# Attention scores in a fused three-layer kernel: from split float32r products to plain float32 in four array tiles

## The reference, cut to what matters

```python
q = proj(hidden_states, Wq, bq) * scaling     # 16 heads of 8
k = proj(hidden_states, Wk, bk)
v = proj(hidden_states, Wv, bv)
scores = jnp.einsum('bhsd,bhtd->bhst', q, k)
scores = scores + chunk_attention_mask(S)[None, None]
probs = jax.nn.softmax(scores, axis=-1)
out = jnp.einsum('bhst,bhtd->bhsd', probs, v)
```

## Time and profile before

| | us |
|---|---|
| median of 3 runs | 1470.39 |
| the profiled execution's own time | 1470.57 |
| its span in the trace | 1468.7 |
| PE busy | 1401.1 (95%) |
| DVE busy | 968.2 (66%) |
| ACT busy | 772.3 (53%) |
| POOL busy | 575.4 (39%) |

### The profile page before, as it was taken

The page is one execution under the profiler, slowest core; times in us unless marked ns, Lnnn a source line. Parts: engine busy times, 40 slices in busy tenths (PEclk is TensorE's granted clock), DMA queues, the critical chain, the costliest instruction groups (busy, mean ns, idle before and its releaser), DMA issues.

```text
span 1468.7 us, 27670 instructions
## 1 busy us (share of the span) xinstructions
PE 1401.1 (95%) x10772; PEld 1220.7 (83%) x10772; DVE 968.2 (66%) x2232; ACT 772.3 (53%) x1043; POOL 575.4 (39%) x517
## 2 busy tenths in 40 slices
PE   4898999999899999999999989999999999999998
PEld 3787878888788888787888878888888888888887
DVE  7666787674766757667575776757755666676543
ACT  6555647553565555636465564555634554355321
POOL 4260655443433553247421672146603431352000
PEclk9899999999999999999999999999999999999999
DMA  7111431104110420152004500061004200500000
GB/s 233 50 31 34 133 76 31 30 8 132 24 46 15 137 40 2 45 139 46 8 2 128 100 1 9 18 165 47 1 1 123 40 2 1 150 13 1 1 8 8
DMA packets 84045, 76.32 MB, mean 52 GB/s; under 512 B 5676, under 2 KB 62044, under 8 KB 83916
## 3 DMA queue, kind: packets, MB, share of 16 engines
q1 hardware_dynamic: 83884, 74.55, 19.3%
q10 hardware_dynamic: 32, 0.02, 0.0%
HBM read 61.69 MB, written 12.85 MB: 51 GB/s over the span
## 4 chain that ended last, share of the span: by engine, by line
PE 75%; DVE 10%; issue 5%; POOL 4%; ACT 3%; DMA 0%; DVEq 0%; POOLq 0%; ACTq 0%
PE pd L1135 25%; PE pg L289 7%; PE pu L289 7%; PE pu L290 6%; PE pu L291 6%; PE pg L291 6%; PE pg L290 6%; PE att_ps L760 3%; DVE h L1244 2%; POOL arena L711 2%; PE att_ps L782 1%; DVE x L1232 1%; POOL arena L713 1%; DVE arena L664 1%; DVE ffn_rows L312 1%
## 5 line engine op out<-in xcount | busy, mean ns | idle before, releaser
L1195 ACT ACTIVATE h<-pg 128x512 f32<-128x512 f32 x512 | 304.1, 597 | 645.1 <-PE pg L291 642.7
L1135 PEld LDWEIGHTS pd<-w_down,h 128*128 128x128 f32 x3840 | 480.3, 192 | 30.1 <-issue 3.6
L1135 PE MATMUL pd<-w_down,h 128*128 128x128 f32 x3840 | 494.6, 277 | 1.2 <-DVE x L1232 1.1
L1244 DVE TENSOR_TENSOR h<-h,pu 128x512 f32<-128x512 f32 x512 | 344.0, 677 | 205.0 <-PE pu L291 194.5
L289 PE MATMUL pg<-ffn_x_hi,w_gate_hi 128*128 128x512 f32 (+1 forms) x544 | 249.7, 459 | 1.1 <-DVE ffn_x_lo L374 1.1
L289 PE MATMUL pu<-ffn_x_hi,w_up_hi 128*128 128x512 f32 (+1 forms) x544 | 210.8, 388 | 19.7 <-DVE h L1244 19.5
L290 PE MATMUL pu<-ffn_x_lo,w_up_hi 128*128 128x512 f32 (+1 forms) x544 | 208.6, 383 | 0.0
L291 PE MATMUL pg<-ffn_x_hi,w_gate_lo 128*128 128x512 f32 (+1 forms) x544 | 208.6, 383 | 0.0
L290 PE MATMUL pg<-ffn_x_lo,w_gate_hi 128*128 128x512 f32 (+1 forms) x544 | 208.5, 383 | 0.0
L291 PE MATMUL pu<-ffn_x_hi,w_up_lo 128*128 128x512 f32 (+1 forms) x544 | 208.2, 383 | 0.0
L971 POOL TENSOR_TENSOR q_weights<-q,pack 128x512 fp32r<-128x512 f32 x136 | 143.8, 1079 | 70.8 <-DMA k<-qk_rows 70.8
(11 more groups left out here) (227 smaller groups left out, 1625.0 us busy)
## 6 DMA issues: line engine op xcount, KB each, us to landing
arena<-bc_spread SPq DMA_DIRECT2D x56, 256.0 KB, 4.7
att_arena<-v_rows SPq DMA_DIRECT2D x64, 144.0 KB, 4.0
qk_rows<-qk_parts SPq DMA_DIRECT2D x32, 256.0 KB, 2.3
q<-qk_rows SPq DMA_DIRECT2D x32, 256.0 KB, 3.7
k<-qk_rows SPq DMA_DIRECT2D x32, 256.0 KB, 4.6
att_arena<-v_rows SPq DMA_DIRECT2D x64, 128.0 KB, 3.4
arena<-in_x SPq DMA_DIRECT2D x8, 256.0 KB, 3.1
x<-in_x SPq DMA_DIRECT2D x8, 256.0 KB, 4.0
```

The lines of the kernel that those rows point to most:

```text
L1135: last = nc.tensor.matmul(pd[:, t * P:(t + 1) * P], h_b[:, d % NH, t * P:(t + 1) * P], wd[:, d % NCH, :], start=d % CPE == 0 and t == 0, s ...
L1195: nc.scalar.activation(h_b[:, c % NH, :], pg[c % 2][:, :], ACT.Silu).then_inc(gate_done, 1)
L1244: nc.vector.tensor_tensor(h, h, pu[d % 2][:, :], ALU.mult).then_inc(h_done, 1)
```

## The change

Q and K are no longer split. ACT writes q and k with bias as plain float32 in their own layout (partition = feature, 8 for each head) and frees the banks. The part on DVE, the DRAM tensor and all DMAs of Q and K go. POOL builds for each window 128x256 in place of 128x512: each partition's query row in eight copies, all but one cleared (head_q). Rows 0 to 63 carry heads 0 to 7, rows 64 to 127 heads 8 to 15. A score matmul takes 64 rows by 64 columns (8 heads' rows, 2 heads x 32 queries) and streams 64 keys in plain float32; the row half b picks the bank, the column half c the partitions. A window has 8 such matmuls, 16 instructions in the trace.

Scores are issued for pairs of units (four windows), ahead of every even unit, and take both att_ps banks at once. The mask add is two instructions, one from each bank, for each unit; the second unit's frees the banks. The mask add and the copy out of the values are now lists of their own on DVE. New places: odd unit's mask 3/8 ahead of its unit, sums 1 1/8, turned 1 5/8, values 1 7/8, copy of the values 2, queries of the next pair 3/8 (even units). The pace is 4.0 in place of 4.1.

```diff
-ATT_PACE = [3.3] + [4.1] * (B - 2) + [3.22]
+S_SC, S_MASK, S_MASK1, S_MAX, S_SUM, S_TURN, S_VAL, S_OUT, S_Q = 1 / 8, 1 / 4, 5 / 8, 3 / 8, 1 / 8, 5 / 8, 7 / 8, 1, 3 / 8
+ATT_PACE = [3.3] + [4.0] * (B - 2) + [3.22]
...
+        NPAIR = -(-NUNIT // 2)
+        PAIRS = [range(4 * m, min(4 * m + 4, NW)) for m in range(NPAIR)]
...
-                def scores(n):
-                    ps = ab.take(pe, ("s", j, n))
-                    pe.wait_ge(q_set, NW * j + UNITS[n][-1] + 1)
-                    for i, w in enumerate(UNITS[n]):
-                        for g in range(4):
-                            last = nc.tensor.matmul(ps[:, (4 * i + g) * WK:(4 * i + g + 1) * WK],
-                                                    q_w[:, n % 2, i, g, :, :].rearrange("p r q -> p (r q)"),
-                                                    k3[:, g, w * WQ:w * WQ + WK], start=True, stop=True)
-                    ab.fill(last, ("s", j, n))
-
-                yield at(1 / 8)
-                pe.wait_ge(qk_moved, 16 * 8 * (j + 1))
+                def scores(m):
+
+                    ps = [ab.take(pe, ("s", j, m, b)) for b in range(2)]
+                    pe.wait_ge(q_set, NW * j + PAIRS[m][-1] + 1)
+                    for i, w in enumerate(PAIRS[m]):
+                        for g in range(2):
+                            for c in range(2):
+                                for b in range(2):
+                                    last = nc.tensor.matmul(
+                                        ps[b][64 * c:64 * c + 64, (2 * i + g) * WK:(2 * i + g + 1) * WK],
+                                        q_w[64 * b:64 * b + 64, m % 2, i, 4 * g + 2 * c:4 * g + 2 * c + 2, :]
+                                        .rearrange("p h q -> p (h q)"),
+                                        k_n[64 * b:64 * b + 64, w * WQ:w * WQ + WK], start=True, stop=True)
+                                    if (g, c) == (1, 1) and w == PAIRS[m][-1]:
+                                        ab.fill(last, ("s", j, m, b))
+
+                yield at(S_SC)
+                ab.wait_free(pe, ("k", j))
                 scores(0)
                 for n in range(NUNIT):
-                    if n + 1 < NUNIT:
-                        yield at(n + 1 + 1 / 8)
-                        scores(n + 1)
-                    yield at(n + 1 + 3 / 4)
+                    if n % 2 and n + 1 < NUNIT:
+                        yield at(n + 1 + S_SC)
+                        scores((n + 1) // 2)
+                    yield at(n + 1 + S_VAL)
...
-                for w, v in enumerate("qk"):
+                for v, to in zip("qk", (q_n, k_n[:, LEFT:LEFT + L])):
                     ab.wait(act, (v, j))
-                    nc.scalar.activation(qk_s[:, w, 0, :], ab.ps((v, j))[:, :], ACT.Identity,
-                                         bias=pk("b_" + v)).then_inc(qk_hi, 1)
+                    ab.free(nc.scalar.activation(to, ab.ps((v, j))[:, :], ACT.Identity, bias=pk("b_" + v)), (v, j))
...
-                yield t0 + 7
-                for w, v in enumerate("qk"):
-                    dve.wait_ge(qk_hi, 2 * j + w + 1)
-                    ab.free(nc.vector.scalar_tensor_tensor(qk_s[:, w, 1, :], ab.ps((v, j))[:, :], pk("b_" + v),
-                                                           qk_s[:, w, 0, :].bitcast(F32), ALU.add, ALU.subtract), (v, j))
...
+            def dve_scores(dve, link, j):
+
+                for n in range(NUNIT):
+                    yield Att.at(j, n + S_MASK1 - 1 if n % 2 else n + S_MASK)
+                    if n >= 2:
+                        dve.wait_ge(p_t, NUNIT * j + n - 1)
+                    nw, m = len(UNITS[n]), n // 2
+                    slot = 0 if n == 0 else 3 if n == NUNIT - 1 else 1
+                    mask = pk("mask").rearrange("p (s k) -> p s k", s=4)[:, slot:slot + nw, :]
+                    for b in range(2):
+                        name = ("s", j, m, b)
+                        ab.wait(dve, name)
+                        ps = ab.ps(name)[:, n % 2 * 4 * WK:(n % 2 * 4 + 2 * nw) * WK]
+                        ps = ps.rearrange("p (w g k) -> p w g k", w=nw, g=2)
+                        ins = nc.vector.tensor_tensor(s_u[n % 2][:, 0:nw, 2 * b:2 * b + 2, :], ps,
+                                                      mask.unsqueeze(2).broadcast_to([P, nw, 2, WK]), ALU.add)
+                        if n % 2 or n == NUNIT - 1:
+                            ab.free(ins, name)
+                        else:
+                            ins.then_inc(s_masked, 1)
...
+            def dve_out(dve, link, j):
+                for n in range(NUNIT):
+                    yield Att.at(j, n + 1 + S_OUT)
...
-                for w, (dst, parts) in enumerate(((q3, (0, 0, 1, 1)), (k3, (0, 1, 0, 1)))):
-                    for i, part in enumerate(parts):
-                        sp.wait_ge(qk_out[w][part], 16 * (j + 1))
-                        at0 = LEFT if w else 0
-                        sp.dma_start(dst[i::4, :, at0:at0 + L].bitcast(F32),
-                                     qk_r[w, part].rearrange("(g e) l -> e g l", g=4)).then_inc(qk_moved, 16)
...
-                def queries(n):
-                    if n >= 2:
-                        ab.wait(pool, ("s", j, n - 2))
-                    for i, w in enumerate(UNITS[n]):
-                        nc.gpsimd.tensor_tensor(q_w[:, n % 2, i, :, :, :],
-                                                q3[:, :, w * WQ:w * WQ + QW].bitcast(F32).unsqueeze(2)
-                                                .broadcast_to([P, 4, 4, QW]), heads, ALU.mult).then_inc(q_set, 1)
+                def queries(m):
+                    nw, w0 = len(PAIRS[m]), PAIRS[m][0] * WQ
+                    if m >= 2:
+                        ab.wait(pool, ("s", j, m - 2, 1))
+                    for i in range(nw):
+                        q = q_n[:, w0 + i * WQ:w0 + i * WQ + QW].unsqueeze(1).broadcast_to([P, 8, QW])
+                        nc.gpsimd.tensor_tensor(q_w[:, m % 2, i, :, :], q, pk("head_q").unsqueeze(2)
+                                                .broadcast_to([P, 8, QW]), ALU.mult).then_inc(q_set, 1)
...
-                    if n + 1 < NUNIT:
-                        yield Att.at(j, n + 1 / 4)
-                        queries(n + 1)
+                    if n % 2 == 0 and n + 2 < NUNIT:
+                        yield Att.at(j, n + S_Q)
+                        queries(n // 2 + 1)
```

More of the change, by code:

```diff
@@ L144, in build @@
         v_d = nc.dram_tensor("v_rows", (NKEY, P), F32, kind="Internal").ap()
-        qk_d = [nc.dram_tensor(f"qk_rows{s}", (2, 2, P, L), F32, kind="Internal").ap() for s in range(2)]
         bc_d = [nc.dram_tensor(f"bc_spread{s}", (2 * DSTATE, L), F32, kind="Internal").ap() for s in range(2)]
@@ L156, in build @@
         with contextlib.ExitStack() as shared:
-            qk_s = shared.enter_context(nc.sbuf_tensor("qk_parts", [P, 2, 2, L], F32R))
+            bc_s = shared.enter_context(nc.sbuf_tensor("bc_parts", [P, 2, 2, L], F32R))
         att_ar = sb("att_arena", [P, N_S + N_V + L + 8])
-        sel = qk_s[0:2 * DSTATE, 0, :, :].rearrange("p a l -> p (a l)")
-        bc_part = [qk_s[0:2 * DSTATE, 1, v, :] for v in range(2)]
+        sel = bc_s[0:2 * DSTATE, 0, :, :].rearrange("p a l -> p (a l)")
+        bc_part = [bc_s[0:2 * DSTATE, 1, v, :] for v in range(2)]
         s_u = [att_ar[:, i * L:(i + 1) * L].rearrange("p (w g k) -> p w g k", w=2, g=4) for i in range(2)]
@@ L188, in build @@
         bt_0 = room[3:5]
-        bc_mid = [[q3[:, k, i * L // 2:(i + 1) * L // 2].bitcast(F32) for k in range(KT)] for i in range(2)]
+        bc_mid = [[q_room[:, k, i * L // 2:(i + 1) * L // 2] for k in range(KT)] for i in range(2)]
         state_mid = sb("state_mid", [P, KT])
@@ L221, in build @@
         y_part, y_done, bc_moved = sem("y_part"), sem("y_done"), [sem("bc_moved0"), sem("bc_moved1")]
-        x_hi, qk_hi, qk_moved = sem("x_hi"), sem("qk_hi"), sem("qk_moved")
-        qk_out = [[sem(f"{v}_{part}_out") for part in ("hi", "lo")] for v in "qk"]
+        x_hi = sem("x_hi")
         v_zero, v_pad, v_out, v_moved, p_t = sem("v_zero"), sem("v_pad"), sem("v_out"), [sem(f"v_moved{i}") for i in range(2)], sem("p_t")
@@ L833, in dve @@
                 ab.free(nc.vector.tensor_copy(attT[:, :], ab.ps(("v", j))[:, :]), ("v", j))
[L835 to L845 removed]
                 def maxima(n):
                     nw = len(UNITS[n])
[L849 removed]
+                    if n % 2 or n == NUNIT - 1:
+                        ab.wait_free(dve, ("s", j, n // 2, 0))
+                        ab.wait_free(dve, ("s", j, n // 2, 1))
+                    else:
+                        dve.wait_ge(s_masked, NUNIT // 2 * 2 * j + n + 2)
                     if j or n:
@@ L871, in turned @@
                                         u.rearrange("p w g k -> p (w g k)")).then_inc(p_t, 1)
-                def out(n):
+                for n in range(NUNIT + 1):
+                    if n:
+                        yield at(n + S_SUM)
```

(28 more changed lines are left out.)

71 lines of the change are left out of this document (10 added, 61 removed).

## The result

1436.8 us, the median of four runs, against 1470.0 for the kernel before in the same session: a ratio of 0.977 (95% interval 0.976 to 0.979), 33 us faster. The forecast was 1454, with a range of 1446 to 1474. The sign was right; the forecast gain, 16 us, was half of what came.

What follows compares the result with a forecast made beforehand. PE, busy 95% of the span, was taken as the bound: 1470.6 - 15.7 (scores) - 1.7 (V's banks) + 1 (new bank wait) = 1454.2, forecast 1454 us, range 1446 to 1474.

Steps and rivals of the forecast that it cites:

- the score term: PE's score matmuls as array tiles: 0.059 us a round, 0.33 us a visit, 15.7 us less for eight sequences.
- rival A: Slower: the row halves of the score tiles take turns, 0.117 us a round, +16 us, 1485 us; chance 13%.
- the value rows: Trace rows of the value products at L782, four column tiles at once, 0.0325 us a round; basis of the score price.
- the rule of the row groups: Trainium skill's rule for PE: a load overlaps a matmul in flight only where the row group differs; halves could only alternate.
- the new wait: PE's score pairs take both att_ps banks, so wait for VectorE's copy of the values: +1 us, bounds nothing to 16 us.
- Rival B: About the same: each pair waits half a microsecond for VectorE's copy, or value products slip; 16 us returned, 1470 us; 12%.
- PE never waits for them, so nothing is gained: POOL's query builds, 512 to 256 columns: about 55 us less of POOL, costed at no gain in time.
- The pace ... at no cost in work: Attention pace 4.0 for 4.1 moves the last unit one chunk forward; costed at nothing.
- nearly, the sum of what PE is given: Outside the first hundred microseconds, time is PE's work; a microsecond off PE in attention is one off the result.
- DVE "even": DVE's load unchanged within 2 us: L827's 11.9 us goes, the two-part mask add costs +9.3 and about +1.2.
- the 1.7 us of V's banks: PE's wait for L827 to free V's banks goes, as ScalarE frees them straight away: -1.7 us.

Runs made afterwards that it cites:

- order_old: The changed kernel with the old places within a unit (sums 1, turned 1 1/2, values 1 3/4, queries 1/4) at pace 4.0: 1453.2 us, ratio 0.9879.
- low_back: The changed kernel with the low parts of Q and K computed on DVE again, into a buffer nobody reads: 1437.3 us, ratio 0.9773.
- dma_back: The changed kernel with the twelve DMAs of Q and K a sequence on SP's queue again, into buffers nobody reads: 1433.6 us, ratio 0.9751.

## Why the prediction was right and wrong

**Right: the score term.** A round costs 0.058 us (forecast 0.059), 68 rounds and five visits a sequence. At 1.28 us for a pair visit and 0.59 for a single one, 32 x 1.28 + 8 x 0.59 = 45.7 us stand against the old 60.9, -15.2 (forecast -15.7). The row halves work side by side, so rival A fell. The choice to go by the value rows rather than by the rule of the row groups was right.

**Right: the new wait, because of where the change put it.** The changed kernel waits 0.2 us for its banks. Rival B's mechanism is real: with the old order PE waits 8.7 us for them. That this order costs 16.4 us as a whole, where the rival had 16, is chance in part, since other waits are in it (`order_old`). The new order avoids the wait; the section on the change lists it, and the prediction did not weigh it.

**Wrong: "PE never waits for them, so nothing is gained", of POOL's query builds.** The price was looked for in PE's waits for POOL. It lies on the way POOL, DVE, PE: POOL's instructions lengthen DVE's, and PE waits for DVE. The halved builds alone take 12.6 us off DVE's busy time and 9.3 us off the kernel before; put back, they cost the changed kernel 10.9. The way there is shown for the kernel before, where DVE's wait for Exp did not fall; in the changed kernel a later subtraction may hold a part. About half of the 9.3 us is idle time of PE (4.1) and half is clock (4.5).

**Wrong: "The pace ... at no cost in work", costed as nothing.** It costs no work, but it moves PE's waits, and with them the stretches at half clock. It alone is 6.1 us in the kernel before, where PE's idle time stays within 1 us and the granted clock goes from 0.990 to 0.994, and 9.1 in the changed one, about half idle time and half clock.

**Wrong: the time as "nearly, the sum of what PE is given".** That step left PE's idle time and its clock as they were. They gave 10.1 and some 4.6 us of the 32.5. The 0.99 of the granted clock stood in the table before, and no term was made of it.

**Wrong: DVE "even".** Its busy time fell by 25 us. L827 took 11.3 of it with it, and the two-part mask add put back 4.8 (44.0 + 3.3 against 48.2 + 3.9); most of the rest is instructions that the change does not touch. `low_back` shows that L827's own load had no cost in time; whether the 1.7 us of V's banks came is below what the times can tell.

The sum in the order of the runs, with medians: 1470.8 before; 1464.6 with the pace; 1461.5 with the new order as well; 1455.9 with half the query columns; 1436.8 with the change whole. The last step of 19.1 us holds the score term, 15.2 us of PE work; the two traces differ by 15.3 us of PE busy time and 3.4 of idle time, at the same granted clock. Which part of the change takes the 3.4 us off was not tested; pairs are a candidate, since the mask adds wait for scores 24 us in place of 36, and the freer queues are not, by `dma_back`. Why the pace of 4.0 is better than its neighbours was settled in part: 4.1 costs idle time and clock, 3.75 and 3.5 cost idle time (6.5 and 11.6 us more). Why PE's waits fall as they do at each pace was not traced. That every unit stands at the same places against the chunks at 4.0 is not shown to be the reason: at 3.5 every second one does, and it was the slowest.

The range failed through its lower end. It was built from bounds on the terms that had a price. The terms costed at nothing, POOL and the pace, had been given no bound below nothing.

## What to carry to other kernels

Price small float32 matmuls in array tiles from any tiled group in the trace, as rounds and visits: two groups of different length give both. Where an engine is said to be off the path, ask which engine's instructions it lengthens, and whether the bound engine waits for that one; a changed mean duration on an untouched line is the sign. Compare the granted clock of every two runs before giving a few microseconds to a cause: here 0.001 of it goes with 1.4 us, and one wait of 2 to 4 us of the bound engine can be paid twice. When two banks are taken at once, look what stands ahead of the copy that frees them on its engine, and after any change of such a list try its pace again.

## What the runs showed of the hardware

- Four tiles of 64 rows by 64 columns in plain float32 work at once: 0.058 us for four instructions, each with a load of 64 weight columns and 64 streamed columns. A visit costs 0.35 us besides (1.28 less 16 rounds), against 0.33 for tiles of 128 by 32.
- Whether neighbours alternate between row halves matters little: 1.14 us for 64 instructions against 1.09.
- DVE instructions with two SBUF inputs take longer beside POOL's work: one mix product of 0.24 us in the mean took 1.98 us and ended with the POOL instruction. The scan took 1528, 1457 and 1349 ns in the kernel before, with half the queries, and in the changed one, but 1396 with POOL as busy as in the kernel before (574 against 575 us), so POOL's load alone does not give the number. The product into h, with an operand in PSUM, stays at 677 to 678.
- PE's granted clock falls to half behind some of its waits: 0.54 over 674 to 680 us behind an idle time of 2.44 us, with float32r matmuls 0.43 us apart in place of 0.23.
